# Attention with scores computed a second time, turned, in place of transposed probabilities

## What is computed

```python
qh = (q @ Wq.T + bq).reshape(b, s, NH, DK).transpose(0, 2, 1, 3)
kh = (k @ Wk.T + bk).reshape(b, s, NH, DK).transpose(0, 2, 1, 3)
vh = (v @ Wv.T + bv).reshape(b, s, NH, DK).transpose(0, 2, 1, 3)
scores = jnp.einsum('bhqd,bhkd->bhqk', qh, kh) / jnp.sqrt(jnp.asarray(DK, qh.dtype))
probs = jax.nn.softmax(scores, axis=-1)
ctx = jnp.einsum('bhqk,bhkd->bhqd', probs, vh)
return concat @ Wo.T + bo
```

## Time and profile before

| | us |
|---|---|
| median of 3 runs | 3006.18 |
| lowest, highest | 2997.04, 3020.54 |
| the profiled execution, its own time | 3021.84 |
| its span, first to last instruction | 3020.2 |

### The profile page before, as it was taken

The page is one execution under the profiler, slowest core; times in us unless marked ns, Lnnn a source line. Parts: engine busy times, 40 slices in busy tenths (PEclk is TensorE's granted clock), DMA queues, the critical chain, the costliest instruction groups (busy, mean ns, idle before and its releaser), DMA issues. The chain is left out here.

```text
span 3020.2 us, 48874 instructions
## 1 busy us (share of the span) xinstructions
PE 2551.7 (84%) x16612; PEld 2263.8 (75%) x16612; DVE 1672.8 (55%) x3170; ACT 1369.7 (45%) x2868; POOL 587.6 (19%) x786
## 2 busy tenths in 40 slices
PE   5888988988898578888888888526999999999996
PEld 4888878887887456767777776425888888888885
DVE  6667766766676347667667575563433433333331
ACT  5445445544554245556556465303444444434342
POOL 1111111111110133333323232102022022021111
PEclk9889989988998689999989899757999999999998
DMA  3100010001000465666646566105243233243221
GB/s 101 36 23 23 22 43 22 22 22 43 22 23 25 116 144 144 146 144 152 145 125 163 131 158 140 35 4 149 85 109 98 92 95 105 73 122 98 80 73 18
DMA packets 229387, 254.30 MB, mean 84 GB/s; under 512 B 65448, under 2 KB 155560, under 8 KB 228624
## 3 DMA queue, kind: packets, MB, share of 16 engines
q1 hardware_dynamic: 188176, 231.16, 28.3%
q0 software_dynamic: 40960, 20.41, 3.9%
HBM read 182.47 MB, written 68.80 MB: 83 GB/s over the span
## 5 line engine op out<-in xcount | busy, mean ns | idle before, releaser
L291 PE MATMUL a_psP<-a_xnT_h,a_win_l 128*128 128x256 f32 x1024 | 318.3, 311 | 14.7 <-DVE a_xnT_l L527 14.5
L1757 PE MATMUL d_psH<-d_xgT_h,d_w_l 128*128 128x308 f32 x1024 | 317.2, 310 | 6.6 <-issue 5.2
L1860 ACT ACTIVATE d_hf<-d_psH,d_b1c 128x308 f32<-128x308 f32 x256 | 130.8, 517 | 410.8 <-PE d_psH L1759 403.6
L1884 DVE TENSOR_TENSOR d_h_l<-d_hf,d_h_h 128x616 fp32r<-128x616 f32 x128 | 102.1, 800 | 382.8 <-ACT d_h_h L1829 382.8
L1758 PE MATMUL d_psH<-d_xgT_l,d_w_h 128*128 128x308 f32 x1024 | 313.3, 306 | 0.0
L1759 PE MATMUL d_psH<-d_xgT_h,d_w_h 128*128 128x308 f32 x1024 | 312.8, 305 | 0.0
L292 PE MATMUL a_psP<-a_xnT_l,a_win_h 128*128 128x256 f32 x1024 | 309.2, 302 | 0.0
L293 PE MATMUL a_psP<-a_xnT_h,a_win_h 128*128 128x256 f32 x1024 | 308.6, 301 | 0.0
L1163 ACT ACTIVATE b_pr<-b_psS,b_nm 128x256 f32<-128x256 f32 x512 | 235.5, 483 | 125.9 <-DVE b_nm L1273 125.9
L599 DVE SCALAR_TENSOR_TENSOR a_v<-a_psP,a_cw,a_v 128x255 f32<-128x255 f32 (+2 forms) x384 | 182.5, 481 | 169.3 <-ACT a_v L474 159.5
L1757 PE MATMUL d_psO<-d_w_h,d_h_l 128*123 128x512 f32 x640 | 253.6, 396 | 9.5 <-DVE d_h_l L1884 9.5
(11 more groups left out here) (316 smaller groups left out, 6384.0 us busy)
## 6 DMA issues: line engine op xcount, KB each, us to landing
d_w<-in_W_dram SPq DMA_DIRECT2D x64, 1024.0 KB, 7.1
b_qst<-qs_d SPq DMA_DIRECT2D x48, 512.0 KB, 9.4
b_kst<-ks_d SPq DMA_DIRECT2D x48, 512.0 KB, 7.0
a_xl<-in_x_dram SPq DMA_DIRECT2D x16, 512.0 KB, 4.3
a_xres<-in_x_dram SPq DMA_DIRECT2D x16, 512.0 KB, 3.9
x_d<-a_xres SPq DMA_DIRECT2D x16, 512.0 KB, 3.1
b_xa<-x_d SPq DMA_DIRECT2D x16, 512.0 KB, 4.0
b_cx<-in_ctxT_dram SPq DMA_DIRECT2D x16, 512.0 KB, 12.2
```

Of the source, the lines that this page charges most:

```text
L291: pe.matmul(out, lo_w, hi_x, start=first, stop=False)
L1757: pe.matmul(out, lo_w, hi_x, start=first, stop=False)
L1860: act.activation(hf[:, m % 2, n * HALF:(n + 1) * HALF], psH[n][:, 0:HALF], ACT.Silu, bias=b1c[par][:, m:m + 1]).then_inc(silu_s, 1)
```

## The change

All of it is in attention_phase. Body b still makes Q, K and V of batch b and the softmax of batch b-1.

- `scores` and `row_max` stay for the row maxima alone. DVE writes the maxima, as high and low parts, in 8 columns (96 to 103) of mxp; `turn_max` transposes them, so that they lie on partitions 96 to 103, one row for each part and head, and `max_rows` (ACT) writes them negated into rows 96 to 103 of qst. The same rows of kst hold ones where a row belongs to the head and zeros elsewhere (sel, written once by POOL).
- `turned` makes the scores a second time with keys on the partitions, over 104 contraction rows, so that the maximum is already taken off. One exponential over 4 heads x 256 queries (1024 columns) writes PT. t_f, pr, rsum, nm, rinv, `norm`, `turn_p` and `pt_copy` go.
- `pv` also multiplies PT with 32 columns of ones, so the sums stand beside the products in psV. `ctx_f` (DVE) takes their reciprocal, 128x256, and multiplies.
- Q and K are split by ACT (`q_hi`) and DVE (`q_lo`) straight from psQ, not by POOL.
- `pv` of the last head group and the output projection of a batch move one body later, and with them the residual and the second layer norm. The projection uses psV alone, the logits psV in place of psQ; `turn_xn` writes psS[1] in place of psT.

The core of the diff follows, indented less. Removed lines are left out: the functions that they belong to stand above.

```diff
+    KR = 3 * DK
+    KX = KR + 2 * G
...
+qst = [sb(f"qst{i}", [KX, H, S], F32R) for i in range(2)]
+kst = [sb(f"kst{i}", [KX, H, S], F32R) for i in range(2)]
 V = [sb(f"V{i}", [P, TT, D]) for i in range(2)]
...
+PT = sb("PT", [P, 2, G, TT, S])
+mx, mxp = sb("mx", [P, TT, G]), sb("mxp", [P, 2, TT, P], F32R)
+cf = sb("cf", [P, S])
...
+            wait(sp, st_mm, U * (b - 1))
             for r, part in enumerate(parts):
                 sp.dma_start(f32(stack[r * DK:(r + 1) * DK, :, :]),
                              f32(scratch[part].rearrange("(h d) s -> d h s", d=DK))).then_inc(ld, 16)
+        if prev2:
+            wait(sp, x2_st, 16 * (b - 2))
+            sp.dma_start(xres[:], x1_v[b - 2]).then_inc(xres_ld, 16)
         if cur and not last(b):
             sp.wait_ge(ln, 7 * b + 7)
...
             wait(sp, q_ld, 48 * b)
             sp.sem_inc(passed_s, 1)
             store(qs_d, tq_st, 0)
+            load(qs_d, tq_st, q_ld, qst[par], (0, 1, 0))
         if prev2:
...
+            sp.wait_ge(x2_s, 2 * (b - 1))
+            sp.dma_start(y_v[b - 2], xres[:]).then_inc(x2_st, 16)
         if cur:
...
             if not last(b):
                 sp.wait_ge(cx_lo, KD * b + KD)
                 sp.dma_start(cx[:], ctx_v[b + 1]).then_inc(cx_ld, 16)
...
             sp.sem_inc(passed_s, 1)
             store(ks_d, tk_st, KD)
             load(ks_d, tk_st, k_ld, kst[par], (0, 0, 1))
...
+        if prev2:
+            sp.wait_ge(ln3, 7 * (b - 1))
+            sp.dma_start(xn3_v[b - 2], xn3[:]).then_inc(xn3_st, 16)
...
+        g.affine_select(out=sel[KR:KX, :], in_=sel[KR:KX, :], compare_op=ALU.not_equal, fill=1.0, base=-G * n,
+                        pattern=[[-1, G]], channel_multiplier=1).then_inc(setup, 1)
+    for i in range(2):
+        pool.wait_ge(setup, 8 + i)
+        g.tensor_copy(kst[i][KR:KX, :, :].rearrange("p (j i) s -> p j i s", i=G),
+                      sel[KR:KX, :].rearrange("p (a i b) -> p a i b", a=1, b=1).broadcast_to([2 * G, KD, G, S])).then_inc(setup, 1)
+    pool.wait_ge(setup, MADE)
...
+                pe.wait_ge(qk_lo, U * b + i)
...
+        def scores(j, qt):
+            n = U * (b - 1) + 2 * j + qt
+            if qt == 0 and j == 0:
+                pe.wait_ge(q_ld, 48 * b)
+                pe.wait_ge(k_ld, 48 * b)
+                wait(pe, exp_s, U * (b - 1))
+            elif qt == 0:
+                pe.wait_ge(mx_s, n - 1)
+            else:
+                wait(pe, mr_s, KD * (b - 1) + j)
+                if j == 0:
+                    pe.wait_ge(xnT_lo, b + 1 if cur else b)
             for h in range(G):
...
+                mm = pe.matmul(psS[qt][:, h, :], qst[o][0:KR, G * j + h, qt * P:(qt + 1) * P],
+                               kst[o][0:KR, G * j + h, :], start=True, stop=True)
             mm.then_inc(s_mm, 1)
...
+        def turn_max(j):
+            pe.wait_ge(ml_s, U * (b - 1) + 2 * j + 2)
+            for qt in range(TT):
+                mm = pe.transpose(psS[1][:, 0, qt * P:(qt + 1) * P], f32(mxp[:, j % 2, qt, :]), ident[:])
+            mm.then_inc(mt_mm, 1)
+        def turned(j, kt):
+            if j == 0 and kt == 0:
+                if isinstance(b, int) and b == 1:
+                    pe.wait_ge(setup, MADE)
+                wait(pe, exp_s, U * (b - 1))
+            elif j == KD - 1 and kt:
+                pe.wait_ge(mx_s, U * (b - 1) + U - 1)
             else:
...
+                pe.wait_ge(exp_s, U * (b - 1) + 2 * j + kt)
+            if kt == 0:
+                pe.wait_ge(mr_s, KD * (b - 1) + j + 1)
+            if j == 2 and kt and prev2:
+                pe.wait_ge(r_cp, b - 1)
+            ps = psS[0] if j == KD - 1 and kt else psT
             for h in range(G):
...
+                mm = pe.matmul(ps[:, h, :], kst[o][0:KX, G * j + h, kt * P:(kt + 1) * P],
+                               qst[o][0:KX, G * j + h, :], start=True, stop=True)
+            mm.then_inc(st_mm, 1)
+        def pv(hb, j, v):
+            pe.wait_ge(exp_s, U * hb + 2 * j + 2)
+            wait(pe, co_lo, KD * hb + j)
             if j == 0:
                 pe.wait_ge(v_cp, 2 * b)
                 wait(pe, x2_s, 2 * (b - 1))
...
+            if j == 2 and prev2:
+                pe.wait_ge(lg_s, b - 1)
+            for half_, w in enumerate((V[v], None)):
+                for kt in range(TT):
+                    for h in range(G):
+                        c = slice((G * j + h) * DK, (G * j + h + 1) * DK)
+                        mm = pe.matmul(psV[h * DK:(h + 1) * DK, half_ * S:(half_ + 1) * S],
+                                       ones[:] if w is None else w[:, kt, c], PT[:, j % 2, h, kt, :],
+                                       start=kt == 0, stop=kt == TT - 1)
             mm.then_inc(pv_mm, 1)
+        def out_proj(t):
...
+        if cur:
+            qk_tile(0)
+        if prev2:
+            pv(b - 2, KD - 1, par)
+        if prev:
+            scores(0, 0)
+        if cur:
+            qk_tile(1)
+        if prev:
+            scores(0, 1)
+        for j in range(3):
+            if prev:
+                scores(j + 1, 0)
             if cur:
...
+                qk_tile(2 * j + 2)
+            if prev:
+                turn_max(j)
+            if prev2 and j == 0:
+                out_proj(0)
+            if prev:
+                turned(j, 0)
+            if prev and j:
+                pv(b - 1, j - 1, o)
+            if prev2 and j == 2:
                 turn_rows()
...
+            if prev:
+                scores(j + 1, 1)
+            if cur:
+                qk_tile(2 * j + 3)
+            if prev2 and j == 0:
+                out_proj(1)
+            if prev:
+                turned(j, 1)
+            if prev2 and j == 2:
                 logits()
         if cur:
             v_tile(0)
         if prev:
...
+            turn_max(KD - 1)
         if cur:
             v_tile(1)
         if prev:
...
+            turned(KD - 1, 0)
+            pv(b - 1, 2, o)
+            turned(KD - 1, 1)
...
+        def q_hi(i):
             act.wait_ge(qk_mm, U * b + i + 1)
...
+            m, n = i % KD, i // KD
+            if m >= 2:
+                act.wait_ge((tq_st, tk_st)[n][m % 2], 64 * b + 32)
+            elif n == 1:
+                act.wait_ge(tq_st[m % 2], 64 * b + 64)
+            else:
+                wait(act, tk_st[m % 2], 64 * b)
+            act.activation(t_h[:, i % 2, :], psQ[:, 0:S], ACT.Identity,
+                           bias=(bqc, bkc)[n][:, m:m + 1]).then_inc(qk_hi, 1)
+        def max_rows(j):
+            act.wait_ge(mt_mm, KD * (b - 1) + j + 1)
+            act.activation(qst[o][KR:KX, G * j:G * j + G, :],
+                           psS[1][KR:KX, 0, :].rearrange("p (o s) -> p o s", o=1).broadcast_to([2 * G, G, S]),
+                           ACT.Copy, scale=-1.0).then_inc(mr_s, 1)
+        def exps(j, kt):
+            act.wait_ge(st_mm, U * (b - 1) + 2 * j + kt + 1)
+            if kt == 0:
+                wait(act, pv_mm, KD * (b - 1) + j - 1)
+            ps = psS[0] if j == KD - 1 and kt else psT
+            act.activation(PT[:, j % 2, :, kt, :], ps[:], ACT.Exp, scale=SCALE).then_inc(exp_s, 1)
+        def ctx_hi(hb, j):
+            act.wait_ge(cf_s, KD * hb + j + 1)
+            wait(act, o_mm, 2 * hb)
+            act.activation(co_h[:, j, :], cf[:], ACT.Identity, bias=bvc[:, j:j + 1]).then_inc(co_hi, 1)
...
+        for u in range(2):
             if cur:
...
+                q_hi(u)
+            if first(b):
                 weights_hi(2 * u + 2)
                 weights_hi(2 * u + 3)
...
+            if prev2 and u == 0:
+                ctx_hi(b - 2, KD - 1)
+        for j in range(3):
+            if cur:
+                q_hi(2 * j + 2)
+            if first(b) and j == 0:
+                weights_hi(6)
+                weights_hi(7)
+            if prev:
+                max_rows(j)
+                exps(j, 0)
+            if prev2 and j == 2:
                 act.wait_ge(r_tp, b - 1)
...
+                copy(xn3T, psT[:], r_cp)
+            if cur:
+                q_hi(2 * j + 3)
+            if prev and j:
+                ctx_hi(b - 1, j - 1)
+            if prev:
+                exps(j, 1)
         if cur:
             v_copy(0)
         if prev:
...
+            max_rows(KD - 1)
         if cur:
             v_copy(1)
         if prev:
...
+            exps(KD - 1, 0)
+            ctx_hi(b - 1, 2)
+            exps(KD - 1, 1)
...
+        def q_lo(i):
+            m, n = i % KD, i // KD
+            dve.wait_ge(qk_hi, U * b + i + 1)
+            dve.scalar_tensor_tensor(out=t_l[:, i % 2, :], in0=psQ[:, 0:S], scalar=(bqc, bkc)[n][:, m:m + 1],
+                                     in1=f32(t_h[:, i % 2, :]), op0=ALU.add, op1=ALU.subtract).then_inc(qk_lo, 1)
+        def row_max(j, qt):
+            n = U * (b - 1) + 2 * j + qt
             dve.wait_ge(s_mm, n + 1)
...
+            wait(dve, ml_s, n - 1)
+            dve.tensor_reduce(mx[:, qt, :], psS[qt][:], AX.X, ALU.max).then_inc(mx_s, 1)
```

(77 more changed lines are left out.)

253 lines of the change are left out of this document (43 added, 210 removed).

## The result

The kernel after takes 3152.8 us, median of 4 runs (3150.78 to 3166.26), the kernel before 3011.6 in the same comparison (4 runs, 2997.04 to 3020.54). The ratio is 1.048, 95% interval 1.043 to 1.054: slower by 141 us, where the forecast was slower by 94 and its range ended at 3145. The profiled execution took 3151.0 (span 3149.4), 129.2 more than the one of before, against the +94 that was worked out for this pair. All of it is in attention: from the first statistics of the layer norm to the end of the last logits it took 936.0 us before (1013.8 to 1949.8) and 1069.7 after (1008.7 to 2078.4), 133.7 more. The phases around it, whose code is the same, took 4.5 less in this pair of executions.

The account below looks back on a forecast made before the run. PE, with waits, was taken to bound a body: 54.4 us going to 59.8, so 70 over 13 bodies, 4.5 for body 15 and 20 for the ends, +94 on 3006, 3100 us. Range 3015 to 3145.

Parts of the forecast that it names:

- ACT's relief: ACT's exponentials and copies in a body: fewer, longer instructions, from 31 us to about 21; ACT nowhere full.
- the walk along PE's order: Changed body followed instruction by instruction on PE at full clock: waits sum to 12.3 us a body, in place of 7.0.
- the latencies: Result latency in a body, another engine starting some 0.13 us after PE's next group, eight times: 1.0 us added.
- The K load's wait: PE's wait for the loaded K stack, 2.7 us today: goes, with 16 us of PE work before its first user.
- the signs of being right: Reciprocals 1.7 to 1.9 us, bodies 58 to 61, PE under 80%, ACT near 21, end gap 4, no kst wait.
- The reciprocal: ctx_f on DVE, 128x256 once per head group: 1.76 us extrapolated from shorter ones, low end 0.42, high end 2.8.
- The rival of the cheap one: Reciprocal of 256 elements costs 0.42 us: bodies +0.9, total +28, 3034 us; chance 0.17.
- The store wait: ACT, not POOL, waits for stores of t_h and t_l at q_hi(6): 0.5 us a body, bounds 0 and 3.
- the half clock: PE at half clock behind the end gap of a body: 1.0 us net, bounds 0 and 3.3 (as now).
- Rival (3): Worse: store wait 3 us and half clock costing as much as now, body 64.6, total 3164 us; chance 0.12.
- The ends: Outside the steady bodies: body 0 +5, body 1 -4, tail +19, together +20 us; body 15, +4.5, counted separately.
- Rival (2): Faster: chain from ctx_f(2) to the split of xn hides beside turned scores, body 50.5, total 2970 us; chance 0.09.

Follow-up runs that it names:

- the filler: 18 unread products of 512 columns added behind turn_xn on PE: against the kernel after, 3142.0 us; a second time on the kernel of products ahead alone, 3133.1 us.
- the tile turned early: Kernel after with turning and splitting of the next xn put ahead of turned(3,0), pv(2) and turned(3,1): 3102.1 us, body 57.8.
- the old start: The kernel of the reciprocal behind the low part, with the start of a body in the order of the kernel after: 3080.2 us, body 57.3.
- the best order: The kernel of xn ahead of the second V tile, with the start of a body in the order of the kernel after: 3019.4 us, ratio 1.001.
- products ahead alone: Kernel after with pv(j-1) ahead of turned(j,0) on PE for j = 1 and 2: 3166.6 us, body 63.0.
- the start reordered: Early turn and products first (3056.2 us), plus first scores ahead of the j = 3 products and their row maximum ahead of that part's reciprocal: 3061.5 us.
- scores ahead of the rows: The kernel of the start reordered, with the last scores (j = 3, second half) ahead of the turn of the rows: 3058.9 us, body 56.5.
- xn ahead of the second V tile: The kernel with the logits behind the first V tile (3035.5 us), with the next tile turned and split ahead of V tile 1: 3063.3 us, ratio 1.015.
- the reciprocal behind the low part: The kernel of xn ahead of the second V tile, with ctx_f of j = 0, 1 behind q_lo(5), q_lo(7), ctx_hi behind the exponentials: 3089.7 us.

## Why the prediction was wrong in its size

**The direction and the mechanism held.** PE got more work and not less, ACT's relief paid nothing (20.4 us a body, 21 forecast), and the new waits came where the walk along PE's order had put them. In the body from 1318.3 to 1379.8: 0.9 and 0.6 at the start (2.1 forecast), 1.5 and 1.6 before the turned scores of groups 1 and 2 (1.3 each), 1.2 before K tile 6 (1.4), 1.4 before the logits (1.4), 0.5 for the V copy (0.4), 4.4 at the end (4.4). With the latencies the waits were forecast at 12.3 + 1.0, and were 12.1. The K load's wait went, as worked out. Of the signs of being right two were missed by a little: bodies of 58 to 61 us (62.4), and PE busy under 80% (80.6).

**The reciprocal** took 1757 ns, the 1.76 extrapolated from the earlier trace rows:

```profile
L1342 DVE RECIPROCAL b_cf<-b_psV 128x256 f32<-128x256 f32 x64 | 112.5, 1757 | 236.1 <-PE b_psV L1073 236.1
```

The rival of the cheap one is gone with this row. The estimate drawn from the Trainium skill ("VectorE: DVE Perf Modes", First, the fixed hardware budget), with its repeat count of 8, would have been 2.3 us. The row shows 6.3 ns for each element beyond the first 32, where that estimate has 8.3, a third too high. The page itself states no time for this instruction.

**The store wait**, taken at 0.5 with bounds 0 and 3, costs PE little. ACT stands for stores of t_l before K tiles for 31.5 us in the 13 bodies, 2.3 to 2.9 at K tile 6 of each. Behind it PE waits 22.3 us in all for the turned scores of group 2, where group 1, which has no such store before it, waits 19.1: 0.25 a body, 0.7 at most.

**The step that failed is the half clock**: "The end gap of 4.4 will do the same, but the stretch behind it is in part DVE's: I take 1.0 net, bounds 0 and 3.3 (as now)." It was 6.2 us a body. The forecast let the term fall from 3.3 to 1.0 while the waits rose from 7.0 to 12.3, and its upper bound was the value of the kernel before, without a reason why twelve microseconds of waits should cost less clock than seven. The rows of before had 3.3 us of half clock beside 7.0 of waits; the same share of 12.3 would have been 5.8. The other terms were a little high (waits and store 13.8 for 12.1, PE's work 45.0 for 44.1), so the body came out at 62.4 for 59.8: 5.2 - 1.7 - 0.9 = 2.6, 34 us over 13 bodies. That these hid half of the error of 5.2 is luck. The 34 are nearly the 35 that lie between 3116, the forecast for the profiled execution, and 3151. Rival (3) had nearly the right total (3164) from the wrong parts: 3 us of store wait that did not come, and 3.3 of half clock where there were 6.2.

That the term is real and not a remainder is shown by the filler: more work on PE, shorter bodies in both pairs, and the clock higher just where the gap was filled. The kernels in which waits went agree: clock 0.94 with the tile turned early, 0.87 where four waits moved together. But the waits alone don't set its size. Between the rows of the table the half clock is 0.36 to 0.70 us for each us of wait, and the two kernels with 9.7 and 9.8 us of waits have 3.5 and 4.1 of it where the one with 8.1 and the old start has 5.7. What exactly makes the clock fall isn't settled.

**The ends.** Body 0, from its first Q tile, cost +3.9 us (56.7 to 60.6, 5 forecast), body 1 -1.2 (-4), body 15 +7.3 (4.5; its granted clock fell from 1.00 to 0.91), the tail +19.2 (19). With 104.7 for the 13 bodies that is the 134 of attention. Bodies 1 and 15 took more than forecast, and the phases around attention 4.5 us less; that these cancel is chance.

**Rival (2)**, faster if the chain from ctx_f(2) to the split hides: the early turn took the end gap away and shortened each body by 4.7, and the best order reached 53.7, not 50.5. Waits for the low parts, before the turned scores and at the start remained. The rival named the right place, and priced it too high.

## What to carry to other kernels

When PE's idle time grows, price it twice: as it stands, and with the half clock behind it. In this kernel 4.6 us more of waits brought 2.4 more of half clock per body, and an estimate that leaves the clock where it was is too low. If nothing better is at hand, take the share of half clock per wait that the trace of before has. A method is to be judged only in an order made for it: the same work, with five calls moved on PE and two on ACT, and DVE's order as it was, was 133 us faster. And after each move see which queue the moved chain now stands in; five of the orders tried (products ahead alone, the start reordered, scores ahead of the rows, xn ahead of the second V tile, the reciprocal behind the low part) gave back elsewhere all that they had saved, or more.

## What the runs showed of the hardware

**Small DVE instructions can last as long as POOL's.** In the kernel with xn ahead of the second V tile, a cast of 128x4 from SBUF to SBUF took 1.13 us and a subtraction of two such tiles 1.22, while POOL added two tiles of 128x512 (2.55 us for the two). Both take 0.17 and 0.16 without that neighbour; the row maximum, which reads PSUM, had its usual 1.21 beside POOL's work on the context. The kernel after has the same thing off its critical path: `ctx_lo`, a 128x256 operation with two SBUF inputs, takes 1.19 us on average the 14 times that it runs beside POOL, and 0.48 the other 50. In the kernel before the same thing happens to the scalings. DVE, then POOL, in one of its bodies:

```profile
1574.61 2.60 DVE L1282 TENSOR_SCALAR b_pr<-b_pr,b_rinv 128x256 f32<-128x256 f32 x4
```
```profile
1574.66 0.40 POOL L942 CAST b_t_h<-b_t_f 128x256 fp32r<-128x256 f32 x1
1575.14 0.72 POOL L944 TENSOR_TENSOR b_t_l<-b_t_f,b_t_h 128x256 fp32r<-128x256 f32 x1
1575.80 0.46 POOL L942 CAST b_t_h<-b_t_f 128x256 fp32r<-128x256 f32 x1
1576.34 0.72 POOL L944 TENSOR_TENSOR b_t_l<-b_t_f,b_t_h 128x256 fp32r<-128x256 f32 x1
```

Four scalings took 2.60 us beside POOL. In the kernel before with the split moved they take 1.14, with POOL idle:

```profile
1574.25 1.14 DVE L1275 TENSOR_SCALAR b_pr<-b_pr,b_rinv 128x256 f32<-128x256 f32 x4
```

The Trainium skill ("GPSIMD Engine Reference", Specifications) says that POOL's SBUF interfaces are shared with VectorE, and that there is contention with instructions that have two SBUF inputs or run in a two-port mode. The subtraction and `ctx_lo` fit the first of these; whether the cast and the scaling run in such a mode no row shows. What the runs add is the size: in these rows a short instruction that starts beside one of POOL's ends 0.02 to 0.15 us behind it.

**A reciprocal of fp32 costs 6.3 ns per further element of a partition** (1757 ns for 256, read from PSUM, and 353 for 32, read from SBUF). For 256 elements that is four times a copy of the same size out of PSUM (0.42 us).
